# The input norm of a graph block, written out with three buffers of x and its statistics taken a group ahead

## What is computed

```python
xn = layernorm(x)
agg[n] = sum over edges e with dst[e] == n of edge_weight[e] * xn[src[e]]
h = relu(((1 + eps) * xn + agg) @ W1.T + b1) @ W2.T + b2
m = mix(xn)             # logmap0, conv to q, k, v, batchnorm over the nodes, attention, conv, expmap0
x = x + h + m
x = x + ffn(layernorm(x))     # only on the N // 2 - 1 nodes with the largest router weight
```

## Time and profile before

| | |
|---|---|
| median of 3 runs | 2685.15 us (2684.79 to 2689.33) |
| the profiled execution | 2689.28 us, of it 2687.7 us span |
| TensorE matmul busy | 2486.6 us, 93% of the span |
| VectorE busy | 1806.8 us, 67% |
| ScalarE busy | 1475.2 us, 55% |
| GpSimd busy | 1766.5 us, 66% |
| DMA, mean | 124 GB/s |

### The profile page before, as it was taken

How to read it: one execution, slowest core, us unless ns; L and a number is a source line. 1 busy time by engine, 2 the same in 40 slices (tenths; PEclk the granted TensorE clock), 3 DMA queues, 4 the chain that set the end, 5 groups by cost and what they waited for, 6 DMA issues and landing times.

```text
span 2687.7 us, 43052 instructions
## 1 busy us (share of the span) xinstructions
PE 2486.6 (93%) x12654; PEld 2176.7 (81%) x12654; DVE 1806.8 (67%) x5986; ACT 1475.2 (55%) x3522; POOL 1766.5 (66%) x1858
## 2 busy tenths in 40 slices
PE   5688899999999999999999999999999999999950
PEld 4566688888888888888888888888888888888840
DVE  5754766767667676676767767676676766767647
ACT  4553555656556565655656556565565656556410
POOL 0006777777777777777777777777777777777500
PEclk9788999999999999999999999999999999999975
DMA  7433444344444434444343443434434344443346
GB/s 220 156 110 97 115 120 125 114 129 116 119 122 118 123 110 119 120 119 119 112 127 113 116 122 113 126 110 118 122 114 124 113 119 118 117 123 112 88 154 231
DMA packets 195536, 333.37 MB, mean 124 GB/s; under 512 B 47838, under 2 KB 138012, under 8 KB 195208
## 3 DMA queue, kind: packets, MB, share of 16 engines
q0 software_dynamic: 85216, 233.60, 30.5%
q1 hardware_dynamic: 105018, 92.42, 10.9%
q10 hardware_dynamic: 5072, 4.57, 0.5%
HBM read 291.99 MB, written 38.46 MB: 123 GB/s over the span
## 4 chain that ended last, share of the span: by engine, by line
PE 78%; DVE 9%; ACT 5%; DMA 5%; issue 1%; ACTq 1%; POOL 1%; SPq 0%; DVEq 0%; POOLq 0%
PE bank L1153 25%; PE qkv L1248 12%; PE bank L1260 12%; PE bank L1167 9%; PE bank L1197 6%; PE qkv L1177 4%; DMA work<-in_x 3%; PE bank L1213 2%; PE qkv L1176 2%; PE bank L1222 2%; PE bank L1187 2%; DMA rings<-xn_dram,window 1%; DVE work L407 1%; ACT work L465 1%; ACT resident L470 1%
## 5 line engine op out<-in xcount | busy, mean ns | idle before, releaser
L772 POOL DMA_INDIRECT rings<-xn_dram,window x1764 | 1753.7, 994 | 675.0 <-issue 375.7
L1153 PE MATMUL bank<-rings 128*128 128x256 f32 x3528 | 891.0, 381 | 19.0 <-DMA rings<-xn_dram,window 15.7
L1153 PEld LDWEIGHTS bank<-rings 128*128 128x128 f32 x3528 | 656.7, 190 | 115.6 <-DVE rings L955 17.2
L955 DVE TENSOR_SCALAR rings<-iota,window_dst,window 128x128 f32<-128x128 f32 x1764 | 562.2, 362 | 164.8 <-PE bank L1153 150.6
L1260 PE MATMUL bank<-ffn_weights,work 128*128 128x256 f32 x1568 | 362.2, 379 | 1.1 <-ACT work L862 1.1
L1248 PE MATMUL qkv<-work,ffn_weights 128*128 128x256 f32 x1568 | 362.3, 379 | 0.7 <-ACT work L855 0.7
L1260 PEld LDWEIGHTS bank<-ffn_weights,work 128*128 128x128 f32 x1568 | 297.9, 190 | 41.9 <-ACT work L862 1.5
L1248 PEld LDWEIGHTS qkv<-work,ffn_weights 128*128 128x128 f32 x1568 | 294.2, 190 | 38.9 <-ACT work L855 0.9
L862 ACT ACTIVATE work<-qkv,fb 128x256 f32<-128x256 f32 x392 | 158.9, 472 | 278.0 <-PE qkv L1248 277.4
L1167 PE MATMUL bank<-resident,weights 128*128 128x256 f32 x1176 | 279.1, 381 | 0.0
L1167 PEld LDWEIGHTS bank<-resident,weights 128*128 128x128 f32 x1176 | 224.5, 191 | 30.8
(11 more groups left out here) (228 smaller groups left out, 3330.1 us busy)
## 6 DMA issues: line engine op xcount, KB each, us to landing
rings<-xn_dram,window POOLq DMA_INDIRECT x1764, 2.8
xn_dram<-work SPq DMA_DIRECT2D x14, 896.0 KB, 7.7
work<-xn_dram SPq DMA_DIRECT2D x49, 256.0 KB
work<-in_x SPq DMA_DIRECT2D x48, 256.0 KB
out<-work SPq DMA_DIRECT2D x48, 256.0 KB
work<-in_x SPq DMA_DIRECT2D x13, 896.0 KB, 5.9
rings<-out SPq DMA_DIRECT2D x5, 896.0 KB, 7.4
out<-rings SPq DMA_DIRECT2D x5, 896.0 KB, 8.1
```

Source lines behind the costliest of these rows:

```text
L772: nc.gpsimd.indirect_dma_start(out=msg[q][:, :], out_offset=None, in_=xn_dram[:, :], in_offset=bass.IndirectOffsetOnAxis(ap=window[t % WIN ...
L955: v.tensor_scalar(sel[k % SEL_RING], iota[:, :], window_dst[b][:, k % SLOTS:k % SLOTS + 1], window[b][:, k % SLOTS, 2:3].bitcast(F32), ALU ...
L1153: te.matmul(agg[h][:, 0:D], sel[k % SEL_RING], msg[q], start=first, stop=last, skip_group_check=True).then_inc(slot_used, 1)
```

## The change

Four things change in the norm stage, and nothing behind it. x has three buffers in place of two, the third in columns of `rings` that are not in use yet, so three loads are issued at the start and load g + 3 is issued when group g is normed. VectorE's step of a group is cut in two, `stats(g)` and `result(g)`, and the program runs `stats(0)`, `stats(1)`, then `result(g)`, `stats(g + 2)` for each g; inside `result` the small operations on the logarithm's argument now stand ahead of the seven writes of the normed tiles. ScalarE takes the seed of g + 1 and the logarithm of g, and then copies tile k of group g - 1 and scales tile k of group g in turn. The parameters are issued by GpSimd, between the parts of `tables_load` and the new `tables_bounds`. The load of `rows` is GpSimd's first instruction, `tables_ends` is VectorE's first work, `tables_chunks` stands behind `result(2)` and `tables_borders` behind `result(4)`. All loops of the norm stage are written out.

```diff
         bounds_ready, bounds_stored, bounds_landed = sem("bounds_ready"), sem("bounds_stored"), sem("bounds_landed")
         bounds_link = sem("bounds_link")
 
-        def tables_load(pool):
+        def tables_rows(pool):
             pool.dma_start(rows[:, :, :].bitcast(I32), dst.rearrange("(c p j) -> p c j", p=P, j=P)
                            ).then_inc(rows_landed, 16)
 
-
+        def tables_load(pool):
             pool.wait_ge(ends_out, 2)
             for k in range(2):
                 pool.dma_start(tile_ends_dram[k], endsT[:EC, k, :]).then_inc(ends_stored, 16)
             pool.wait_ge(ends_stored, 32)
             pool.dma_start(ends_bc[:NT], tile_ends_dram.rearrange("k c j -> k (c j)").partition_broadcast(NT)
                            ).then_inc(ends_landed, 16)
+
+        def tables_bounds(pool):
             pool.wait_ge(border_ready, 1)
             for k in range(2):
                 nc.gpsimd.indirect_dma_start(
@@ -185,12 +187,12 @@
...
             pool.dma_start(bounds[:, :], bounds_dram.rearrange("t k -> (t k)").rearrange("(a n) -> a n", a=1)
                            ).then_inc(bounds_landed, 16)
 
-        def params_act(act):
+        def params_pool(pool):
             def load(dst_ap, src_ap):
-                act.dma_start(dst_ap, src_ap).then_inc(params_landed, 16)
+                pool.dma_start(dst_ap, src_ap).then_inc(params_landed, 16)
 
             load(wqkvT, a["wqkvT"][2].rearrange("(c p) o -> p c o", p=P))
-            act.wait_ge(consts_ready, N_CONST)
+            pool.wait_ge(consts_ready, N_CONST)
             for g in range(4):
                 load(mixW[32 * g:32 * g + 32, :, 32 * g:32 * g + 32], a["w_pw"][g])
             load(wresT, a["wresT"].rearrange("(c p) o -> p c o", p=P))
@@ -297,7 +299,6 @@
         bounds_link2, rem_counted = sem("bounds_link2"), sem("rem_counted")
 
...
         def tables_tensor(pe):
-            pe.wait_ge(h0T_ready, 4 * G)
             pe.wait_ge(ends_ready, 1)
             for k in range(2):
                 nc.tensor.transpose(banks[k][0:EC, 0:P], ends[:, k, :], ident[:, :]).then_inc(ends_turned, 1)
@@ -311,23 +312,23 @@
 
 
 
-        xb = [view(work, 1792 * h, G, D) for h in range(2)]
+        xb = [view(work, 0, G, D), view(work, 1792, G, D), view(rings, 11 * D, G, D)]
         xnb = [view(work, 3584 + 1792 * h, G, D) for h in range(2)]
         hb = [view(work, 7168 + 1792 * h, G, D) for h in range(2)]
         st = [view(work, 10752 + 150 * h, 150) for h in range(2)]
-        x_landed = [sem(f"x_landed{h}") for h in range(2)]
+        x_landed = [sem(f"x_landed{h}") for h in range(3)]
...
-        norm_link = sem("norm_link")
+        norm_link, stats_link = sem("norm_link"), sem("stats_link")
...
         def norm_sync(sp):
-            load(0, 0)
-            load(1, 1)
-            with sp.Fori(0, NG // 2 - 2) as u:
-                for h in range(2):
-                    sp.wait_ge(xn_ready, u * 2 + (h + 1))
-                    load(u * 2 + (h + 2), h)
-                    store(u * 2 + h, h)
-            sp.wait_ge(xn_ready, NG - 3)
...
+            def load(g):
+                if g < NG - 1:
+                    sp.dma_start(xb[g % 3], node_rows(x, g * G, G)).then_inc(x_landed[g % 3], 16)
+                else:
+                    sp.dma_start(xb[g % 3][:, 0:G - 1], node_rows(x, g * G, G - 1)).then_inc(x_landed[g % 3], 16)
+                    sp.wait_ge(xlast_clear, 1)
+                    sp.dma_start(xb[g % 3][0:LAST, G - 1], x[(NT - 1) * P:N, :]).then_inc(x_landed[g % 3], 16)
+
+            def store(g):
+                sp.dma_start(node_rows(xn_dram, g * G, G), xnb[g % 2]).then_inc(xn_stored[g % 2], 16)
+
+            for g in range(3):
+                load(g)
+            for g in range(NG):
+                sp.wait_ge(xn_ready, g + 1)
+                if g + 3 < NG:
+                    load(g + 3)
+                store(g)
...
-        def norm_vector(dve, stats_turn):
+        def norm_vector(dve):
             v = nc.vector
...
+
+            def stats(g):
+                h = g % 2
+                link = Link(dve, stats_link, 1, g)
+                part, mv, var = view(st[h], 0, G, 6), view(st[h], 42, G, 2), norm_cols(h)[0]
+                dve.wait_ge(x_landed[g % 3], 16 * (g // 3 + 1) + (16 if g == NG - 1 else 0))
+                for k in range(G):
+                    ins = v.bn_stats(part[:, k], xb[g % 3][:, k])
+                ins.then_inc(stats_ready, 1)
+                dve.wait_ge(stats_ready, g + 1)
+                for k in range(G - 1):
+                    v.bn_aggr(mv[:, k], part[:, k])
+                link(v.bn_aggr(mv[:, G - 1], part[:, G - 1]))
+                v.tensor_scalar(var[:, 0], mv[:, :, 1], LN_EPS, None, ALU.add)
+                v.tensor_scalar(var[:, 1], mv[:, :, 1], TINY, None, ALU.add).then_inc(var_ready, 1)
+                link.close()
+
+            def result(g):
+                h = g % 2
                 link = Link(dve, norm_link, NORM_LINKS, g)
-                stats = view(st[h], 0, G, 6)
...
                 dve.wait_ge(rsqrt_seed, g + 1)
                 newton(v, link, y, var, t)
-                if before is not None:
-                    dve.wait_ge(xn_stored[h], before * 16)
-                    dve.wait_ge(h0_ready, before * (2 * G) + (h - 1) * G)
-                for k in range(G):
-                    ins = v.tensor_scalar(xnb[h][:, k], xb[h][:, k], mv[:, k, 0:1], y[:, 0, k:k + 1],
-                                          ALU.subtract, ALU.mult)
-                ins.then_inc(xn_ready, 1)
-
                 v.tensor_tensor(t[:, 0], var[:, 1], y[:, 1], ALU.mult)
                 link(v.tensor_tensor(t[:, 1], var[:, 0], y[:, 0], ALU.mult))
                 v.scalar_tensor_tensor(num, t[:, 0], float(D) ** 0.5, y[:, 0], ALU.mult, ALU.mult)
+                if g >= 2:
+                    dve.wait_ge(xn_stored[h], 16 * (g // 2))
+                    dve.wait_ge(h0_ready, (g - 1) * G)
                 link(v.scalar_tensor_tensor(s0, t[:, 1], float(D) ** -0.5, y[:, 1], ALU.mult, ALU.mult))
                 link(v.tensor_scalar(num, num, 1e-15, BALL, ALU.max, ALU.min))
                 link(v.tensor_scalar(den, num, -1.0, 1.0, ALU.mult, ALU.add))
                 link(v.reciprocal(den, den))
                 v.scalar_tensor_tensor(num, num, 1.0, den, ALU.add, ALU.mult).then_inc(ln_in, 1)
+                for k in range(G):
+                    ins = v.tensor_scalar(xnb[h][:, k], xb[g % 3][:, k], mv[:, k, 0:1], y[:, 0, k:k + 1],
+                                          ALU.subtract, ALU.mult)
+                ins.then_inc(xn_ready, 1)
                 dve.wait_ge(ln_out, g + 1)
                 v.scalar_tensor_tensor(s0, ln, 0.5, s0, ALU.mult, ALU.mult).then_inc(s0_ready, 1)
                 link.close()
 
-            step(0, 0, 16, None)
-            step(1, 1, 16, None)
-            step(2, 0, 32, 1)
-            step(3, 1, 32, 1)
-            step(4, 0, 48, 2)
             tables_ends(dve)
-            step(5, 1, 48, 2)
-            tables_chunks(dve)
...
-            dve.reg_mov(stats_turn, 7)
-            with dve.Fori(3, NG // 2 - 1) as u:
-                step(u * 2, 0, u * 16 + 16, u)
-                step(u * 2 + 1, 1, u * 16 + 16, u)
-            v.memset(xb[1][:, G - 1], 0.0).then_inc(xlast_clear, 1)
-            step(NG - 2, 0, 16 * (NG // 2), NG // 2 - 1)
-            step(NG - 1, 1, 16 * (NG // 2 + 1), NG // 2 - 1)
+            stats(0)
+            stats(1)
+            for g in range(NG):
+                result(g)
+                if g == NG - 4:
+                    dve.wait_ge(xn_ready, NG - 3)
+                    v.memset(xb[(NG - 1) % 3][:, G - 1], 0.0).then_inc(xlast_clear, 1)
+                if g == 2:
+                    tables_chunks(dve)
+                if g == 4:
+                    tables_borders(dve)
+                if g + 2 < NG:
+                    stats(g + 2)
...
-            def step(g, h):
-
-                rsqrt_table(g + 1, 1 - h)
+            rsqrt_table(0)
+            for g in range(NG):
+                if g + 1 < NG:
+                    rsqrt_table(g + 1)
+                log(g)
                 for k in range(G):
-                    copy(g, k)
-                    if k == 2:
-                        log(g + 1, 1 - h)
-                    if k >= G - 3:
-                        for m in range(2 * (k - (G - 3)), 2 * (k - (G - 3)) + 2):
-                            scale(g + 1, 1 - h, m)
-                scale(g + 1, 1 - h, G - 1)
-
-            rsqrt_table(0, 0)
-            log(0, 0)
-            for k in range(G):
-                scale(0, 0, k)
-            step(0, 0)
-            with act.Fori(0, NG // 2 - 1) as u:
-                step(u * 2 + 1, 1)
-                step(u * 2 + 2, 0)
+                    if g > 0:
+                        copy(g - 1, k)
+                    scale(g, k)
             for k in range(G):
                 copy(NG - 1, k)
...
-            step(0, 0, True)
```

(7 more changed lines are left out.)

80 lines of the change are left out of this document (25 added, 55 removed).

## The result

The changed kernel takes 2667.54 us in the median of 4 runs (2663.26 to 2668.95), the kernel before 2685.86 (4 runs, 2684.79 to 2689.33). The medians differ by 18.3 us. The ratio, taken run against run, is 0.9927, with a 95% interval of 0.991 to 0.9944: faster, by 15 to 24 us. Forecast were 2652.7 us in a range of 2646 to 2666. The sign was right; the gain was a little over half of the 32.5 us forecast, and the time lies 1.5 us above the range. The profiled execution took 2668.47 us; before it was 2689.28.

What follows compares the result with a forecast made beforehand. Norm groups were held by engines waiting in a ring, none full. First `s0` 27.3, 13 groups of 7.6 and tables 17.7 put the last Gram product at 156, 32.5 us earlier: 2656.8 profiled, less 4.1 gives 2652.7, range 2646 to 2666.

Steps and rivals of the forecast that it cites:

- What bounds the kernel, and the steady groups: Norm stage: no engine full; a group falls from 9.6 to 7.6 us, gaining 26 us over 13 groups.
- The ring of waits: Norm's steady groups: TensorE, VectorE and ScalarE wait for each other, one group following another after 10.03 us.
- The start: Norm's beginning: rows land at 10.7, first `s0` at 27.3 us, 0.6 earlier, with `tables_ends` and a set of statistics done.
- What is hidden, and its cover: GpSimd's 21 parameter issues: free within 48 us, 2.3 us each, before `border_ready`; their 4.4 MB share transfers at 20 to 50.
- x comes late: Rival, loads of x: landing at 10 us costs 1.35 a group, 15 over eleven loads; 2668 us, chance 0.15.
- The other price that I named for this move: GpSimd's descriptor writes locked out by VectorE's two-port modes: at most 2.2 us, or some 30 us for 21 issues, within 48.
- The tables: VectorE between groups: `tables_chunks` 10.1 and `tables_borders` 7.7 us, 17.7 again; the 1.2 us wait for the spread table goes.
- The sum: End of norm: last `s0` at 143.8, last Gram product at 156 against 188.5, 32.5 us earlier.
- TensorE's stop ahead of that point: TensorE at `tables_borders`: stands about 3 us, after about 8 in `tables_chunks`.
- 4 us for the lower clock: TensorE returning from a table stop: four tiles at 1.2 GHz cost 4 us, kept to the end.
- The term for TensorE's delay: Last Gram product: 4 us added, from 152.1 to 156, as TensorE's 7.59 a group is no shorter than VectorE's.
- this offset: Whole time: median taken 4.1 us below the profiled execution, from 2656.8 to 2652.7.

Runs made afterwards that it cites:

- e6: Changed kernel with stats(g) directly ahead of result(g) and ScalarE's seed of g ahead of the logarithm of g; main stage begins at 213.14 us, changed kernel 187.51.
- e1: Changed kernel with GpSimd issuing the 21 parameters only after result(2); main stage begins at 180.00 us, ratio to the kernel before 0.9899.
- e4: Changed kernel with the parameters issued by ScalarE again, ahead of its first instruction; main stage begins at 178.88 us, ratio to the kernel before 0.9933.
- e2: Changed kernel with SyncE holding load 7 and store 4 until the two indirect loads landed; their wait 4.21 us, ratio to the kernel before 0.9911.
- e3: Changed kernel with 36 unneeded products of zeros on TensorE ahead of groups 3 and 5; last Gram product 2.7 us earlier, ratio to the kernel before 0.9927.
- e5: Changed kernel with two buffers of x instead of three; 2722.83 us in one run, against 2684.10 for the kernel before.
- e9: Changed kernel with parameters issued after result(2), indirect loads two groups ahead, stats(0) and stats(1) ahead of tables_ends; 2644.32 us, ratio to the kernel before 0.9854.
- e8: Changed kernel with parameters after result(2), indirect loads two groups ahead, 36 zero products ahead of group 3; slower chip, ratio to the kernel before 0.9861.
- e7: Changed kernel with parameters issued after result(2) and indirect loads two groups ahead; main stage begins at 167.93 us, ratio to the kernel before 0.9905.
- e0: Changed kernel unedited, on a slower chip; main stage begins at 187.22 us against 187.51, ratio to the kernel before 0.9919.

## Why the prediction fell short

**What bounds the kernel, and the steady groups: right.** The ring of waits was the cause of the 10 us groups, and the statistics and the seed a group ahead break it (7.47 against 7.60 forecast; 10.71 in e6, which undoes both). TensorE had nothing to spare, as said, and was the engine without a stop from 94.8 us on.

**The start: right within 0.7 us.** First `s0` at 28.0, forecast 27.3; the rows landed 1 us later than assumed.

**What is hidden, and its cover: this is the step that failed.** I wrote that the 4.4 MB now share the transfer engines with x and the stores in 20 to 50 us, and that "`tables_chunks` gives a pause of 10 us in the middle of it". I checked the cover for GpSimd's issues (it held: 13 us for 21, done at 33.8) and not the cover for what they set going. Load 3 is issued at 28.1 and wanted at 35.7, ahead of `tables_chunks`, not behind it. The rival "x comes late" had the mechanism, but I priced it as a landing time common to all loads, at 10 us and 1.35 a group. It was one load, at 15.3 us, and cost 7.83 us. e1 takes only this away, and its last Gram product comes 7.7 us earlier; e4 undoes the move of the issues and gains 6.4 there. The other price that I named for this move, GpSimd held up by VectorE's `tensor_scalar`, is real and small (last section), and did not come into the sum.

**The tables: mis-sized.** I took 4.18 us for the indirect loads as before. Before, they had the transfer engines for themselves (DMA share 0.04 from 90 to 100 us); after, `border_ready` comes right behind `result(4)`, which also releases load 7 and store 4. The wait is 7.52; e2 shows that it is these two transfers.

**The sum, redone.** TensorE runs without a stop from `s0` of group 5 on. Forecast, that was 27.3 + 5 x 7.6 + 17.7 = 83.0; measured, 94.0. Of the 11.0 us, 0.7 are the start, 7.8 x of group 3, 3.1 the tables, and the groups give 0.7 back. TensorE's stop ahead of that point was 8.58 us where I had about 3. Behind it I had 4 us for the lower clock, and it was 2.7 (71.0 us for 63 tiles of 1.085; e3 gives back 2.7). So the last Gram product came at 165.8 in place of 156, and the gain up to the main stage was 23.0 us and not 32.5. The term for TensorE's delay was right in kind. One slip had no effect: the last group has no statistics behind it, so VectorE had 3.2 us less to do than I counted (1.1 us of it showed, for it then waited 2.0 for the last logarithm), but TensorE set the end.

**Behind the norm.** The batchnorm stage is as long as before (21.7 against 22.0 us), as forecast. The profiled executions differ by 20.8 us and the medians by 18.3, less than 23.0. The main stage took 2477.2, 2479.4, 2477.4 and 2475.5 us in the four profiled executions on such chips (before, changed, e5, e9). The 2 to 5 us between lie within what runs of one kernel differ by, and within the interval; nothing here ties them to the change. The forecast took 4.1 us off the profiled execution to get the median; here the median lies 0.9 below it. So of the 14.8 us between forecast and result, 9.5 are the norm's, 2.2 came behind the batchnorm and 3.2 are this offset, for which nothing here shows a cause. With 4.1 again the time would have been 2664.4, inside the range by luck and with the same failed step.

## What to carry to other kernels

When an issue of transfers is moved, ask two questions of its cover: when the issuing engine must be free, and which other transfer is in flight with the moved bytes and when that is wanted. A load that lands in 5.9 us with 1.4 us of slack has none beside 4.4 MB of weights. In a pipeline in which all engines need nearly the same time, the end is the last stop of the engine with the least to spare plus its work from there on. What ends that stop earlier counts in full, an early wait of another engine too (e1); an early stop of that engine filled by itself does not, and can make a later one longer (e8).

## What was not expected of the hardware

The issue of 21 transfers took GpSimd 13.0 us, 0.62 each and none over 0.9, where ScalarE needed 20.6 with one of 3.19. In e1 one of them was longer, and it ran beside a `tensor_scalar` of VectorE over 1664 elements (GpSimd's and VectorE's timelines):

```profile
48.15 1.26 POOL L192 DMA_DIRECT2D weights<-in_W2T  x1
```
```profile
48.17 1.09 DVE L267 TENSOR_SCALAR resident<-resident,rings 98x1664 f32<-98x1664 f32 x1
```

The same issue took 0.74 us in the changed kernel, where VectorE had no instruction of that length beside it; here it ended 0.15 us behind VectorE's instruction. e7, e8 and e9 have it as well (1.27, 1.27 and 1.28 us). So VectorE can hold up an issue of GpSimd, by 0.5 us in these cases.

The same burst of transfers made very different waits: 15.3 us for the load issued in the midst of them in the changed kernel, 6.7 us for one issued 0.3 us ahead of them in e1, and 17.1 us for the store issued just behind the first of them there. TensorE's stops of 1.47 and 1.72 us ended at the upper clock, and those of 3.80 and 8.58 at the lower (first row 0.69 us in place of 0.44); but in e5 one of 2.67 ended at the lower and one of 3.07 at the upper, and in e0 one of 4.14 at the upper, so the length of the stop alone does not say it. In the batchnorm stage of e7 the clock fell with no stop at all. And two chips took the same 187 us up to the main stage and then 2479 and 2828 for it. On the slower one the list of waits names a releaser, `remote`, that the faster one has nowhere; what it stands for, no run here shows:

```profile
ACT work L768 <- remote: 277.5, 44, 10.6
...
DVE work L342 <- issue: 95.9, 37, 4.0
```
